# Causal masks of the four layers: from mask matmuls to copies that ScalarE writes into PSUM ahead of the scores

## The reference

```python
L, H, NH, NKV, HD, FF, E, K = (4, 128, 16, 4, 64, 256, 8, 2)
def _attention(x, wq, wk, wv, wo, cos, sin, causal_bias):
    ...
    q = q * c + _rot_half(q) * sn
    k = k * c + _rot_half(k) * sn
    k = jnp.repeat(k, rep, axis=1)
    v = jnp.repeat(v, rep, axis=1)
    scores = jnp.einsum('bhqd,bhkd->bhqk', q, k) / jnp.sqrt(jnp.asarray(HD, x.dtype))
    scores = scores + causal_bias
    attn = jax.nn.softmax(scores, axis=-1)
    out = jnp.einsum('bhqk,bhkd->bhqd', attn, v)
    out = out.transpose(0, 2, 1, 3).reshape(b, s, NH * HD)
    return out @ wo
causal_bias = jnp.where(jnp.tril(jnp.ones((s, s), bool))[None, None], 0.0, -1000000000.0)
for l in range(L):
    h = _rms(x, ln1_w[l])
    h = _attention(h, wq[l], wk[l], wv[l], wo[l], cos, sin, causal_bias)
    x = jnp.clip(res + h, -100.0, 100.0)
    ...
    h = _moe(h, wr[l], wg[l], wu[l], wd[l])
    x = jnp.clip(res + h, -100.0, 100.0)
```

## Time and profile before

| | |
|---|---|
| median of 3 runs | 3364.86 us (3364.7 to 3366.26) |
| the profiled execution, its own time | 3365.88 us |
| its span | 3364.0 us |
| busy PE / PEld / DVE / ACT / POOL | 3165.4 / 2097.7 / 2568.0 / 1706.8 / 2009.9 us |
| mask matmuls of the maxima (L1757) | 704 |
| mask matmuls of the scores (L1785) | 256 |
| HBM read, written | 88.47 MB, 31.72 MB |

### The profile page before, as it was taken

The page is one execution under the profiler, slowest core; times in us unless marked ns, Lnnn a source line. Parts: engine busy times, 40 slices in busy tenths (PEclk is TensorE's granted clock), DMA queues, the critical chain, the costliest instruction groups (busy, mean ns, idle before and its releaser), DMA issues.

```text
span 3364.0 us, 51431 instructions
## 1 busy us (share of the span) xinstructions
PE 3165.4 (94%) x17792; PEld 2097.7 (62%) x17792; DVE 2568.0 (76%) x3764; ACT 1706.8 (51%) x3085; POOL 2009.9 (60%) x1573
## 2 busy tenths in 40 slices
PE   5999998799999999999999999999999999999998
PEld 3555554566666677666666776666667766666576
DVE  6778775777887777878876778778867888788667
ACT  4566667444435475444344755443446553443465
POOL 2101000378778665778776657787776577876765
PEclk8899999899999999999999999999999999999999
DMA  5433412333322155332231553232215532232153
GB/s 121 78 67 62 81 45 43 77 85 68 75 61 67 46 172 134 82 73 64 67 73 32 181 138 85 61 76 67 61 30 188 141 90 61 67 76 61 27 175 116
DMA packets 160401, 283.60 MB, mean 84 GB/s; under 512 B 32592, under 2 KB 64208, under 8 KB 159888
## 3 DMA queue, kind: packets, MB, share of 16 engines
q1 hardware_dynamic: 159632, 280.18, 33.4%
q10 hardware_dynamic: 512, 0.13, 0.0%
HBM read 88.47 MB, written 31.72 MB: 36 GB/s over the span
## 4 chain that ended last, share of the span: by engine, by line
PE 52%; DVE 6%; ACT 3%; issue 2%; POOL 1%; DMA 1%; SPq 0%; DVEq 0%; ACTq 0%
PE psA L1799 11%; PE psA L1782 7%; PE psA L1754 6%; PE psA L1783 5%; PE psA L1826 3%; PE psA L1827 3%; PE psA L1828 3%; PE psA L1814 3%; DVE rden L2084 2%; PE psA L1821 2%; DVE mxp L2110 2%; PE psA L1863 1%; PE psA L1757 1%; PE psA L1864 1%; PE psA L1865 1%
## 5 line engine op out<-in xcount | busy, mean ns | idle before, releaser
L1415 ACT ACTIVATE prob<-psA 128x512 f32<-128x512 f32 x1152 | 652.6, 595 | 1045.6 <-PE psA L1783 460.2
L1217 POOL TENSOR_TENSOR xw<-xw,prob 128x512 f32<-128x512 f32 x672 | 867.9, 1291 | 232.3 <-ACT prob L1415 158.5
L2110 DVE TENSOR_REDUCE mxp<-psA 128x1 f32<-128x512 f32 (+3 forms) x864 | 528.5, 663 | 57.1 <-PE psA L1754 35.2
L2084 DVE RECIPROCAL rden<-psA 128x256 f32<-128x256 f32 x256 | 448.8, 1753 | 131.9 <-PE psA L1814 125.5
L1782 PE MATMUL psA<-qs,ks 128*128 128x512 f32 x1152 | 524.8, 456 | 18.7 <-ACT prob L1415 17.4
L1754 PE MATMUL psA<-ks,qs 128*128 128x512 f32 (+3 forms) x1536 | 476.6, 387 | 11.8 <-DVE mxp L2110 5.7
L1251 POOL TENSOR_TENSOR hidl<-gate,hidh 128x512 fp32r<-128x512 f32 x256 | 331.2, 1302 | 211.4 <-ACT hidh L1470 209.6
L1783 PE MATMUL psA<-qs,ks 128*128 128x512 f32 x1152 | 454.6, 395 | 0.0
L1217 POOL TENSOR_TENSOR xw<-prob 128x512 f32<-128x512 f32 x224 | 287.7, 1284 | 274.0 <-issue 129.8
L2032 DVE TENSOR_REDUCE mxp<-psA 128x1 f32<-128x1024 f32 x256 | 304.7, 1220 | 83.7 <-PE psA L1590 82.7
L1334 ACT ACTIVATE pr<-psA 128x512 f32<-128x512 f32 x512 | 274.3, 602 | 140.1 <-PE psA L1609 122.9
(11 more groups left out here) (222 smaller groups left out, 5839.0 us busy)
## 6 DMA issues: line engine op xcount, KB each, us to landing
qs<-normed SPq DMA_DIRECT2D x256, 256.0 KB, 4.1
rbp<-rab SPq DMA_DIRECT2D x256, 192.0 KB, 3.5
spread<-routing_weights SPq DMA_DIRECT2D x128, 256.0 KB, 3.6
qs<-qs SPq DMA_DIRECT2D x64, 256.0 KB, 3.2
expert_weight_halves<-eh SPq DMA_DIRECT2D x32, 384.0 KB, 2.5
expert_weight_halves<-el SPq DMA_DIRECT2D x32, 384.0 KB, 3.6
eh<-expert_weight_halves SPq DMA_DIRECT2D x32, 384.0 KB, 3.2
el<-expert_weight_halves SPq DMA_DIRECT2D x32, 384.0 KB, 3.9
```

What stands on the lines that cost most here:

```text
L1217: g.tensor_tensor(psum_k[:, t % 2, :], before, prob[:, i % 4, :], ALU.add).then_inc(s_su, 1 if kt > 1 else 2 + (t == 1))
L1415: act(prob[:, k % 4, :], psS[:, k % 2, :], ACT.Exp, scale=float(HD) ** -0.5).then_inc(s_ex, 1)
L2084: vec.reciprocal(rden[:, :], psO[t % 2][:, 256:512]).then_inc(s_rd, 1)
L2110: vec.tensor_reduce(dst, bank, AX.X, ALU.max).then_inc(s_mr, 1)
```

## The change

For a piece of the maxima that ends in the diagonal tile, ACT copies `maskq` into the bank before the scores' matmuls, which then add up on it (no matmul of the piece starts the bank anew); the mask matmul is left out. `maskq` becomes 512 columns wide, zeros and then the mask, and the copy writes the last k1 - k0 columns of it for each head of the piece: 512 or 384 columns in all. `SEEDED` holds these pieces: those with a bank whose item before was not a "J" and not none. Eight pieces in a layer are left with the matmul. For a diagonal step of the scores ACT copies `maskk` into the `psS` bank, four times 128 columns. The copies are steps of their own in the plan ("Mz", "Sz") with their costs, and the PE steps wait for them. The projections' first matmul starts the bank anew as before, and of a pair of value projections in one bank only the first does so. `skip_group_check=True` is an argument of the matmul call and adds no instruction.

```diff
+def diagonal(t, m):
+    return max_pieces(t)[m][3] == (t + 1) * P
+SEEDED = {item: None for item in EARLY + MAIN if item[0] == "M" and diagonal(*item[2:]) and BEFORE[item] and BEFORE[item][0] != "J"}
+SEEDED = {item: i for i, item in enumerate(SEEDED)}
...
-            stage("tensor", ("M", l, n, t, m), w * max(115, (k1 - k0) / 2.2) + (90 + w * 35) * (k1 == (t + 1) * P), ("land", ("Q", l, n, t // TPC)),
-                  ("vector", ("K", l, n, t // TPC)), *turn)
+            seeded = ("M", n, t, m) in SEEDED
+            if seeded:
+                stage("scalar", ("Mz", l, n, t, m), 230 + 0.75 * w * (k1 - k0), *turn)
+                turn = [("scalar", ("Mz", l, n, t, m))]
+            stage("tensor", ("M", l, n, t, m), w * max(115, (k1 - k0) / 2.2) + (90 + w * 35) * (diagonal(t, m) and not seeded),
+                  ("land", ("Q", l, n, t // TPC)), ("vector", ("K", l, n, t // TPC)), *turn)
...
-        stage("tensor", ("S", l, n, t, kt), 440 + 100 * (kt == t), ("land", ("J", l, n, t // TPC)) if kt == 0 else None,
-              back("scalar", "S", 2), *first)
+        if kt == t:
+            stage("scalar", ("Sz", l, n, t), 610, back("scalar", "S", 2), *first)
+            first = [("scalar", ("Sz", l, n, t))]
+        stage("tensor", ("S", l, n, t, kt), 440, ("land", ("J", l, n, t // TPC)) if kt == 0 else None, back("scalar", "S", 2), *first)
...
-        maskq = sb("maskq", [P, P], BF16)
+        maskq = sb("maskq", [P, 512], BF16)
...
+                elif what == "Mz":
+                    l, n, t, m = i
+                    was, of, *part = BEFORE["M", n, t, m]
+                    it = l * HEADS + of
+                    if was == "W":
+                        a.wait_ge(s_vs, NT // 2 * l + of + 1)
+                    elif was == "P":
+                        a.wait_ge(s_rp, 2 * (3 * (it * NCH + part[0]) + part[1] + 1))
+                    else:
+                        a.wait_ge(s_mr, it * N_MAXED + PIECES[part[0]] + part[1] + 1)
+                    _, w, k0, k1 = max_pieces(t)[m]
+                    act(banks[BANK["M", n, t, m]][:, 0:w * (k1 - k0)].rearrange("p (h n) -> p h n", h=w),
+                        maskq[:, 512 - (k1 - k0):512].unsqueeze(1).broadcast_to([P, w, k1 - k0]), ACT.Copy).then_inc(s_mz, 1)
+                elif what == "Sz":
+                    l, n, t = i
+                    k = TRI[t] + t
...
+                    a.wait_ge(s_ex, (l * HEADS + n) * TRI[TPB] + k + 3)
+                    act(psS[:, k % 2, :].rearrange("p (h n) -> p h n", h=GQ), maskk[:, :].unsqueeze(1).broadcast_to([P, GQ, P]), ACT.Copy).then_inc(s_sz, 1)
...
-                vacant(l, ("M", n, t, m))
+                seed = SEEDED.get(("M", n, t, m))
+                if seed is None:
+                    vacant(l, ("M", n, t, m))
+                else:
+                    t_.wait_ge(s_mz, l * len(SEEDED) + seed + 1)
...
-                             start=(i == 0), stop=not diagonal)
-                if diagonal:
+                             start=(i == 0 and seed is None), stop=not masked, skip_group_check=True)
+                if masked:
...
+                if kt == t:
+                    t_.wait_ge(s_sz, it * TPB + t + 1)
                 tile = slice(kt * P, (kt + 1) * P)
-                mm(psS[:, i % 2, :], ks[b][:, 0, tile], qs1[b][:, c, :, qs], start=True, stop=False)
-                ins = mm(psS[:, i % 2, :], ks[b][:, 1, tile], qs2[b][:, c, :, qs], start=False, stop=(kt < t))
-                if kt == t:
-                    ins = mm(psS[:, i % 2, :], identb[:, :], maskk[:, :].unsqueeze(1).broadcast_to([P, GQ, P]), start=False, stop=True)
-                ins.then_inc(s_qk, 1)
+                mm(psS[:, i % 2, :], ks[b][:, 0, tile], qs1[b][:, c, :, qs], start=(kt < t), stop=False, skip_group_check=True)
+                mm(psS[:, i % 2, :], ks[b][:, 1, tile], qs2[b][:, c, :, qs], start=False, stop=True, skip_group_check=True).then_inc(s_qk, 1)
```

More of the change, by code:

```diff
@@ L841, in program @@
         s_rw = [sem(f"max2_in_stack_{c}") for c in range(NCH)]
+        s_mz, s_sz = sem("max2_mask_in_psum"), sem("scores2_mask_in_psum")
         s_qk, s_ex, s_su, s_pv = sem("scores2"), sem("exp2"), sem("probabilities_summed"), sem("pv2")
@@ L1608, in opening @@
                         t_.wait_ge(s_ex1, k - 2)
-                    mm(psS1[:, k % 3, :], kst[r][0:121, h, kt * P:(kt + 1) * P], qst[r][0:121, c, h, :], start=True, stop=True).then_inc(s_qk1, 1)
+                    mm(psS1[:, k % 3, :], kst[r][0:121, h, kt * P:(kt + 1) * P], qst[r][0:121, c, h, :], start=True, stop=True,
+                       skip_group_check=True).then_inc(s_qk1, 1)
                 elif what == "V":
@@ L1735, in project_values @@
                     dst = banks[BANK["W", j]][:, k * NKV * HD:(k + 1) * NKV * HD]
-                    mm(dst, xh[:, ts], wvh[:, :], start=True, stop=False)
+                    mm(dst, xh[:, ts], wvh[:, :], start=(k == 0), stop=False)
                     mm(dst, xh[:, ts], wvl[:, :], start=False, stop=False)
-                    ins = mm(dst, xl[:, ts], wvh[:, :], start=False, stop=True)
+                    ins = mm(dst, xl[:, ts], wvh[:, :], start=False, stop=(k == 1))
                 ins.then_inc(s_vp, 1)
@@ L1751, in maximum @@
                 bank = bank[:, 0:w * (k1 - k0)].rearrange("p (h n) -> p h n", h=w)
-                diagonal = k1 == (t + 1) * P
+                masked = diagonal(t, m) and seed is None
                 for i in range(w):
                     ins = mm(bank[:, i, :], qs1[b][:, c, h + i, t % TPC * P:(t % TPC + 1) * P], ks[b][:, 0, k0:k1],
-                             start=(i == 0), stop=not diagonal)
-                if diagonal:
-                    ins = mm(bank[:, :, k1 - k0 - P:k1 - k0], identb[:, :], maskq[:, :].unsqueeze(1).broadcast_to([P, w, P]),
-                             start=False, stop=True)
+                             start=(i == 0 and seed is None), stop=not masked, skip_group_check=True)
+                if masked:
+                    ins = mm(bank[:, :, k1 - k0 - P:k1 - k0], identb[:, :], maskq[:, 512 - P:512].unsqueeze(1).broadcast_to([P, w, P]),
+                             start=False, stop=True, skip_group_check=True)
                 ins.then_inc(s_ms, 1)
```

20 lines of the change are left out of this document (12 added, 8 removed).

## The result

The changed kernel takes 3,341.05 us, the kernel before 3,364.78 in the same comparison: ratio 0.9934, 95% interval 0.9917 to 0.9951. It is faster by 0.7%, 23.7 us. The forecast was 3,277, 88 us faster. The wide range of 3,205 to 3,385 held the time. The forecast's own range, 3,235 to 3,325, did not, and the gain is about a quarter of what was forecast.

The account below looks back on a forecast made before the run. PE, busy 97% of layer 1's main stretch, was taken as the bound. Slots of 151.5 us, less 56 for copy delays and 8 for other engines, gave 87.5 us: 3,277 us, own range 3,235 to 3,325, wide range 3,205 to 3,385.

Parts of the forecast that it names:

- In the place that is edited PE sets the pace, and an instruction taken from PE is worth its slot on PE: Layer 1's heads 1 to 7: PE busy 97% of 425 us, so removed mask matmuls give their full slots, 151.5 us.
- 12 us in the stretch: PE's stalls in layer 1's main stretch of 425 us, each expected to become somewhat longer.
- The slots themselves (0.125 and 0.23 us): PE time per narrow 128-column mask and per score mask, read from start-to-start distances in the timeline.
- The estimate by the Trainium skill's figure: Alternative price of the removed mask matmuls, 55.6 ns per narrow one: 105 us instead of 151.5; not adopted.
- ACT's work as free: The 928 mask copies add 523 us on ACT, which has room; nothing charged for their sum, only for delay.
- The delay of the copies: Waits caused by score and maxima copies, 60 and 24 us, taken at two thirds: 56 us given back.
- 60 of 84 us to the score copies: Diagonal score steps: a third of 256 delayed by the full 0.7 us, as the copy must follow an earlier exp.
- PE waits in only 44 of 1,216 piece starts: Row maxima, four banks turning over: 5% of 672 copies delayed by 0.7 us, 24 us.
- I put no more than 2 us a layer: DVE and POOL have less room once PE does less, so PE's stalls lengthen: 8 us charged in all.
- The pace goes to DVE and POOL: Rival, chance 0.15: three quarters of the gain lost in these engines' queues, 38 us stay, about 3,327 us.
- The copy is on the path of each diagonal step: Rival, chance 0.15: score steps wait for copies in ACT's queue; slower, 3,398 us, at worst some 3,460.
- all of it: Rival, chance 0.17: all copies hide and PE gives its full 151.5 us, so 3,213 us.

## Why the prediction was wrong

**"In the place that is edited PE sets the pace, and an instruction taken from PE is worth its slot on PE": this step failed.** It rested on PE being busy 97% of the stretch and on a chain made of PE lines. The direction held: masks out is faster. The price did not: 159 us of slots were worth 57 in place, 36%, and 55 us were to be had without touching PE. The rows that spoke of it were there. 5.9% of the chain were the reciprocal; I named it and priced it at nothing. And the text itself said that a matmul's 0.39 us are not its slot of 0.23, yet read the busy share of 97% as if they were. The stalls that I put at "12 us in the stretch" could only be those longer than that overlap.

**The slots themselves (0.125 and 0.23 us) hold.** Over all places of this kind in the trace they are 0.12 to 0.21 and 0.23 us; that PE's busy time fell by 107 us for 159 is no measure of them. The estimate by the Trainium skill's figure (TensorE: Matmul & The Clock Gate, "Wait — 56ns, not 53.3ns?"), 105 us, would have been nearer to the outcome and for the wrong reason: its 55.6 ns for a narrow mask is less than half of what these places show, it too prices a slot as time, and the missing part lies in waits that appear elsewhere.

**ACT's work as free: nearly right.** ACT was busy 458 us longer, and 555 us of copies made aside cost 9.5 us.

**The delay of the copies: 56 us in the sum, 37 measured**, so by itself the term was somewhat too dear. For the two kinds alone it was split the wrong way. I gave 60 of 84 us to the score copies, because they stand between two exps on two banks. PE waited 5 times, 3 us, for a score copy; alone they cost nothing that the total shows. The maxima's, which I gave 24 since "PE waits in only 44 of 1,216 piece starts", gave back all of their gain: a copy waits for DVE at the head of ACT's queue, and I had read only how PE waits. In the changed kernel's own order the split is the other way round, 24 and 13, and nearly half of the 24 (11 us) is the wait for the routing, which I had not priced.

**"I put no more than 2 us a layer" on the lost room of the other engines: this term of 8 us is where the missing 100 us belonged** (159 us of slots, 57 to 62 us of gain without any copy). The rival *The pace goes to DVE and POOL* was the nearest, at 3,327 with a chance of 0.15, though its mechanism was not met either: neither engine went above 81%. Not an engine's sum but waits between engines in a fixed order took the gain. *The copy is on the path of each diagonal step* did not come; *all of it* would have needed a kernel that waits for nothing.

**Two slips in the working.** Delays of 24 to 106 us give 3,245 to 3,327, not the "3,235 to 3,325" that the text names; the measured time is outside both. And of the two gaps of ACT that it put down to PE coming late, the row of the longer one, 2.75 us, says "issue": ACT waited for nothing that the profile shows.

**The clock**: the forecast kept it. The mean granted clock fell by 0.003; the stretches of 3.4 us at half clock behind the longer idle pieces of PE are a further loss of at most about 7 us.

## What to carry to other kernels

On an engine that is busy 97%, what you take away can be worth a third of its slots. Before summing slots, shorten one thing on each neighbour (here the reciprocal and the sum to a quarter) and see what the time says; it is one line each, and the answer here was 55 us for DVE and 13 for POOL. A wait that moves to another engine's queue is priced by what it holds up there, not by how often the first engine waited. And where a list scheduler lays the order, compare an edit in the order that stands as well as in the new one: an order alone moved one of these programs by about 65 us, nearly three times the change.

## Not expected

- Two complete programs with the same instructions and the same count of matmul records (16,832) took 3,306 and 3,371 us. Leaving the maxima's masks out altogether, with the old order and no copies, took 3,332, less than the changed kernel.
- 555 us of copies on ACT, made beside everything else, cost 9.5 us. Into SBUF, bf16 to bf16, a 512-column copy took 626 to 628 ns, a little more than the 597 to 600 into PSUM.
- Plan costs nearer to the measured durations made the order worse by about 20 us once and changed nothing once. Why is left open; no run takes the planner's other constants one by one.
- With bf16 in and f32 out, a copy of 512 columns into PSUM took 597 to 600 ns, the same as the exp's 593 from PSUM in that kernel. The Trainium skill (ScalarE: Activation LUTs, "What ACT_TABLE_LOAD costs") gives 186 ns + 0.833 ns per column for an ACTIVATE with immediate operands, which comes to 613 ns for 512 columns and 506 for 384; the trace has 597 to 600 and 487, so the rule is within 4%.
